# Two reordered instruction streams: GpSimd splits chunks 3, 5 and 7 ahead of weight sums, ScalarE casts chunk 3 ahead of the first gelu

## The reference, cut to what matters

```python
# layer 0: a weight mixed per sequence from 8 masked ones
w_bot = einsum('bg,got->bot', cond, weight * mask)
x = x + einsum('bnt,bot->bno', x, w_bot) + bias
# layer 1: top 2 of 8 by softmax(cond), and the shared expert
def mlp(x, gate_w, up_w, down_w):
    return (gelu(x @ gate_w) * (x @ up_w)) @ down_w
x = x + sum_e w[b, e] * mlp(x, expert e) + mlp(x, shared)
```

## Time and profile before

| | |
|---|---|
| median of 3 runs | 414.45 us (414.2 to 414.62) |
| the profiled execution | 414.13 us, of which 412.3 us are the span from the first to the last instruction |
| TensorE busy | 407.1 us (99% of the span), granted clock 1.000 |
| VectorE, ScalarE, GpSimd busy | 305.4, 253.1, 313.3 us (74%, 61%, 76%) |
| DMA | 35.23 MB, mean 85 GB/s |

### The profile page before, as it was taken

The page is one execution under the profiler, slowest core; times in us unless marked ns, Lnnn a source line. Parts: engine busy times, 40 slices in busy tenths (PEclk is TensorE's granted clock), DMA queues, the critical chain, the costliest instruction groups (busy, mean ns, idle before and its releaser), DMA issues.

```text
span 412.3 us, 7445 instructions
## 1 busy us (share of the span) xinstructions
PE 407.1 (99%) x2241; PEld 354.9 (86%) x2241; DVE 305.4 (74%) x511; ACT 253.1 (61%) x484; POOL 313.3 (76%) x322
## 2 busy tenths in 40 slices
PE   8999999999999999999999999999999999999997
PEld 6778888888988888888888888988888889888886
DVE  4787897586768887866777879866687677677784
ACT  6586767675555568655555567757555557675541
POOL 1699999999709679999634879999680986999730
PEclk9999999999999999999999999999999999999999
DMA  8552443333100522243000253222300042232201
GB/s 266 201 171 77 135 122 78 101 90 103 43 24 2 166 89 79 90 142 102 28 25 2 49 180 102 76 76 82 96 25 25 0 129 76 76 111 72 51 0 53
DMA packets 19616, 35.23 MB, mean 85 GB/s; under 512 B 2179, under 2 KB 2947, under 8 KB 19587
## 3 DMA queue, kind: packets, MB, share of 16 engines
q1 hardware_dynamic: 19296, 34.61, 27.3%
q10 hardware_dynamic: 290, 0.26, 0.2%
HBM read 32.77 MB, written 2.10 MB: 85 GB/s over the span
## 4 chain that ended last, share of the span: by engine, by line
PE 96%; DVE 1%; ACT 1%; issue 0%; POOL 0%; DVEq 0%; POOLq 0%
PE o_ps L549 16%; PE p_ps L549 12%; PE g_ps L495 10%; PE g_ps L494 10%; PE g_ps L498 10%; PE u_ps L495 10%; PE u_ps L494 10%; PE u_ps L498 10%; PE l_ps L450 2%; PE g_ps L620 1%; PE u_ps L413 1%; PE p_ps L431 0%; PE o_ps L589 0%; DVE u_ps L985 0%; DVE out_sb L1067 0%
## 5 line engine op out<-in xcount | busy, mean ns | idle before, releaser
L1166 POOL TENSOR_TENSOR eg_lo<-raw_g,eg_hi 128x512 fp32r<-128x512 f32 x64 | 88.5, 1404 | 11.2 <-ACT eg_hi L691 11.2
L720 ACT ACTIVATE gelu<-g_ps 128x512 f32<-128x512 f32 x95 | 57.0, 600 | 57.5 <-PE g_ps L498 56.2
L990 DVE SCALAR_TENSOR_TENSOR u_ps<-gelu,route_cur,u_ps 128x512 f32<-128x512 f32 x64 | 48.1, 751 | 52.4 <-PE u_ps L498 49.8
L1026 DVE TENSOR_TENSOR h_lo<-t_raw,h_hi 128x1024 fp32r<-128x1024 f32 x46 | 80.9, 1759 | 0.2 <-ACT h_hi L753 0.2
L740 ACT CAST h_hi<-u_ps 128x256 fp32r<-128x256 f32 x46 | 17.2, 373 | 60.1 <-DVE t_raw L1005 42.8
L1208 POOL TENSOR_TENSOR ed_lo<-s_raw,ed_hi 128x512 fp32r<-128x512 f32 x30 | 52.7, 1757 | 0.0
L495 PE MATMUL g_ps<-x_hi,eg_lo 128*128 128x512 f32 (+1 forms) x128 | 50.3, 393 | 0.0
L1206 POOL TENSOR_TENSOR ed_lo<-raw_d,ed_hi 128x384 fp32r<-128x384 f32 x30 | 39.4, 1313 | 14.3 <-ACT ed_hi L700 14.1
L494 PE MATMUL g_ps<-x_hi,eg_hi 128*128 128x512 f32 (+1 forms) x128 | 50.1, 391 | 0.0
L495 PE MATMUL u_ps<-x_hi,eg_lo 128*128 128x512 f32 (+1 forms) x128 | 49.8, 389 | 0.0
L494 PE MATMUL u_ps<-x_hi,eg_hi 128*128 128x512 f32 (+1 forms) x128 | 49.8, 389 | 0.0
(11 more groups left out here) (226 smaller groups left out, 1154.3 us busy)
## 6 DMA issues: line engine op xcount, KB each, us to landing
raw_g<-experts SPq DMA_DIRECT2D x64, 256.0 KB, 2.8
raw_d<-experts SPq DMA_DIRECT2D x32, 256.0 KB, 2.7
l_raw<-l_w SPq DMA_DIRECT2D x8, 256.0 KB, 5.1
x_in<-xT SPq DMA_DIRECT2D x8, 256.0 KB, 4.0
raw_g<-shared SPq DMA_DIRECT2D x8, 256.0 KB, 4.2
outT<-out_sb SPq DMA_DIRECT2D x6, 256.0 KB, 3.3
raw_d<-shared SPq DMA_DIRECT2D x4, 256.0 KB, 2.9
mask<-l_mask SPq DMA_DIRECT2D x2, 128.5 KB, 5.5
```

Source lines behind the costliest of these rows:

```text
L720: act.activation(gelu[:, s % 2], l0_ps if at_first(b) and s == 1 else g_ps, ACT.Gelu_apprx_tanh).then_inc(gelu_done, 1)
L990: dve.scalar_tensor_tensor(u_ps[:, s % 2], gelu[:, s % 2], route_cur[:, k:k + 1], u_ps[:, s % 2], ALU.mult, ALU.mult).then_inc(h_done, 1)
L1026: dve.tensor_tensor(h_lo[:, at], t_raw[:], h_hi[:, at].bitcast(F32), ALU.subtract).then_inc(t_lo_done, 1)
L1166: pool.tensor_tensor(eg_lo[:, j % RING], raw_g[:, j % RAW_G], eg_hi[:, j % RING].bitcast(F32), ALU.subtract).then_inc(gu_lo_done, 1)
```

## The change

Only orders change; no instruction is added or taken away. On ScalarE the cast of chunk 3 moves from behind `copy_b12` to ahead of gelu 0, the 384-column down cast of pair 0 from ahead of gelu 0 to behind it, and the cast of `s_raw` of pair 0 from ahead of `copy_b12` to behind the casts of the hidden values of pair 0. On GpSimd `shared_s(0)` moves from between the halves of chunk 1 to behind the split of chunk 3, which itself moves ahead of the down split of pair 0; chunk 5 is split ahead of the sums of pair 2, and chunk 7 ahead of those of pair 3.

```diff
@@ ScalarE, weights_beside
                 if at_first(b):
-                    if s == 0:
-                        split_shared(FIRST)
                     if s % 2:
@@ ScalarE, main order
             split_gate(2)
             split_up(2)
+            split_shared(FIRST)
+            activate(0, 0)
             split_shared_d(0)
-            activate(0, 0)
-            split_shared_s(0)
             copy_b12(0, 0)
-            weights_beside(0, 0)
             activate(0, 1)
             split_b11(0, 0)
             split_b2(0, 0)
+            split_shared_s(0)
             first_x1(0)
             weights_beside(0, 1)
             first_x1(1)
@@ GpSimd, batch_0
                 split_gate(1)
-                shared_s(0)
                 split_up(1)
                 split_gate(2)
                 split_up(2)
+                split_shared(FIRST)
+                shared_s(0)
                 split_shared_d(0)
-                split_shared(FIRST)
                 for s in range(1, STEPS):
                     if s % 2:
                         p = (s + 1) // 2
+                        if s in (3, 5):
+                            split_shared(chunks_at(s)[0])
                         if p < PAIRS:
                             shared_s(p)
                         elif p < NP:
                             expert_s(0, p - PAIRS)
-                        for c in chunks_at(s):
+                        for c in chunks_at(s)[1 if s in (3, 5) else 0:]:
```

## The result

The changed kernel takes 414.92 us (median of 19 runs, 414.32 to 415.81) against 414.38 us (19 runs, 413.94 to 415.76) of the kernel before: a ratio of 1.0014, 95% interval 1.0008 to 1.0021, that is 0.33 to 0.87 us longer. 415.25 us had been predicted, +0.80 us. By the time alone the first rival, 414.87 us, lies nearer; what tells it from the forecast are the profiles.

A forecast was written before the change was run, and what follows sets the result against it. TensorE, 96% of the chain, was taken as the bound, every delay ahead of step 3's gate reaching the end. 0.51 + 0.29 = +0.80 us on 414.45 gave 415.25 us, range 414.3 to 416.0.

The forecast's parts named there:

- first rival: VectorE's last routing instruction is not caught by GpSimd's chunk 3: +0.42 us, 414.87 us; chance 0.20.
- Part 1: ScalarE's cast of chunk 3 leaves the chain ahead of gelu 1: gain at most 0.09 us.
- Part 2: ScalarE's cast of s_raw enters the chain between hidden cast and x1, ahead of gelu 2: +0.51 us.
- Part 3: VectorE's last routing instruction waits behind GpSimd's chunk 3 split, delaying the second product: +0.29 us, replacing the cast's gain.
- Part 4: GpSimd's later splits and sums, though delayed, stay ahead of TensorE's matmuls: costs nothing, wins nothing.

The follow-up runs named there:

- E5: Changed kernel with gelu 2 ahead of the two x1 copies and chunk 4's cast on ScalarE; ratio 0.9997 to the kernel before.
- E6: Kernel before with gelu 2 ahead of the two x1 copies and chunk 4's cast on ScalarE; ratio 1.0000 to the kernel before.
- E8: Changed kernel with gelu 2 early and VectorE's last four routing instructions behind the first two products; ratio 0.9988 to the kernel before.
- E2: Changed kernel with GpSimd's sums of pair 0 back between the halves of chunk 1; ratio 1.0004 to the kernel before.
- E3: Changed kernel with ScalarE's cast of s_raw of pair 0 between the two hidden casts, not behind them; ratio 1.0005 to the kernel before.
- E4: Changed kernel with VectorE's last four routing instructions behind the first two products and their splits; ratio 1.0004 to the kernel before.
- E10: Kernel before with gelu 2 early, chunks 5 and 7 ahead of their sums, and last four routing instructions behind the first two products; ratio 0.9982.
- E7: Kernel before with only chunks 5 and 7 split ahead of the sums of pairs 2 and 3; ratio 1.0002 to the kernel before.
- E1: The changed kernel unaltered, timed and profiled once more; ratio 1.0014 to the kernel before.

## Why the prediction was right

**The place.** It said that every delay ahead of the gate of step 3 reaches the end. Shown: in the changed kernel the shift is the same at that gate and at gate 5 (0.81 and 0.80 us), and the rest of the span is constant within 0.24 us over twelve profiles. It holds for time that is added. Time that is won reached the end only up to the next bound (E5, E6, E8).

**Part 1**, gain of at most 0.09 us: gelu 1 is behind the copy at once; the gain shows nowhere, since part 3 takes its place, as said. In E2, where it could show, the second product starts at 3.90 us instead of 3.93, so some 0.03 us were won, not 0.09. The second product starts 0.10 us behind the end of the up of step 1 there (21.45 + 0.62 = 22.07, then 22.17), where the prediction had put 0.04. That is why 0.48 us stayed there where 0.42 had been expected.

**Part 2**, +0.51 us: measured +0.51 in ScalarE's rows; E3 takes 0.47 of it back.

**Part 3**, +0.29 us: measured +0.30 at the second product; E2 and E4, two different ways to take it away, give 0.33 us both. The two ways of undoing it leave the second product where TensorE's up of step 1 ends, 3.90 us behind the reference matmul, so they take back the gain that part 1 left open too (0.30 + 0.03). The three instructions were each caught by the GpSimd instruction that the prediction named; the last of them (L918, now L916), forecast to end 0.81 us later than before, ended 20.91 - 18.22 = 2.69 us behind the reference matmul against 19.69 - 17.82 = 1.87 (+0.82). The sentence on the Trainium skill ("SBUF — State Buffer", section "Who interferes with whom": with two SBUF inputs against a GpSimd read, the second to issue blocks for the whole instruction) is borne out by 1.22 us of the last routing instruction, which has two SBUF inputs, and again in E10. The 0.62 us that the prediction gave with it as agreeing are no case of this rule as put: the second instruction (L916 before, L914 now) reads one SBUF tile, `pair`, and was held up all the same, 0.62 and 0.66 us.

**Part 4**, nothing: no wait on `sg_lo` in the changed kernel. Chunk 4's split was forecast to be done by 28.4, or 29.7 if held up once; it took 2.28 us and ended at 29.87, 29.47 with the later start taken off. Chunk 5's slack, forecast to grow from 0.14 us by more than 1 us, is 34.69 - (32.07 + 1.28) = 1.34 us. The remark that there is nothing to win at chunk 5 held for this kernel (E7), but the first stall was hiding a second one: once it is removed, E6 shows a wait of 0.84 us on chunk 5.

**The size.** 0.80 us by profile, 0.54 us by the medians of the timed runs, whose interval of 0.33 to 0.87 us holds both. E1's timed medians give 0.58 us, again below its profile's 0.81. What lies between them was not settled. The 19 runs of the changed kernel scatter by 1.5 us and those of the kernel before by 1.8, and the start of the reference matmul alone by 0.97 us over the twelve profiles. So it may be scatter, or in some of the timed runs VectorE's last routing instruction is not caught by chunk 3; the four profiles with the sums late and the routing instructions in their place (changed, E1, E3, E5) all show it caught, and nothing on record tells of the timed runs beside them. So the mechanism rests on the profiles, and the timed runs agree with it without proving its size.

## What to carry to other kernels

Where one engine has 96% of the chain, look for its few gaps and list what stands in order ahead of each; moving a cast of 0.5 us into such a list cost all of it here, and moving instructions out of it (the x1 copies behind the gelu) won only up to the next bound, which had to be lifted in the same edit. A VectorE instruction of a few columns was not small where GpSimd was busy: the routing instructions on SBUF tiles took what was left of GpSimd's instruction, and a chain of three dependent ones met three in turn. So look at what runs beside such a chain; beside sums of 128 columns each link took 0.35 to 0.38 us (E4, E8). Where the scatter of runs is above the effect, compare intervals between two instructions of one profile: they repeated within 0.01 us in the kernel that was profiled twice. And count a wait from start to start of TensorE's matmuls: the idle time printed was 0.83 us where 1.01 us could be won.

## What the runs showed of the hardware

- The mutual exclusion works both ways. In the changed kernel GpSimd's chunk 4 was issued at 27.59, behind VectorE's split of the t values, and took 2.28 us instead of 1.30:

```profile
27.43 1.28 DVE L1024 TENSOR_TENSOR h_lo<-t_raw,h_hi 128x1024 fp32r<-128x1024 f32 x1 [0.24 <-ACT h_hi L753]
```

- In the kernel before chunk 4 was first (25.59), and the same split of VectorE, issued at 26.21, took 1.76 us instead of 1.28.
- The length of the wait is not a matter of an instruction's size: the three routing instructions on 8 columns took from 0.17 us (L914 before) to 1.22 us, and all those of 0.35 us and more ended 0.02 to 0.03 us behind GpSimd's instruction.
- Not every VectorE instruction was held up. The reciprocal took 0.16 us beside GpSimd's gate half at 18.20. The product, with one input in PSUM, took 0.68 us beside a half split (19.61 in the kernel before) and beside sums (20.83 in the changed one).
- TensorE's idle time of 1.35 us ahead of the gate of step 3 did not lower its granted clock, which is 1.00 (2.4 GHz) from 14 to 25.25 us and from 26.6 to 60 us in the changed kernel.
